# Gated attention with a mixture of experts: three sets of chunks instead of five share their blocks, waits that another wait covers are left out, and VectorE adds four diagonals in every chunk

## The reference

```python
# x, ctx: (128, 64, 128), 8192 tokens of D = 128
def _L0_xattn_ref(q, k, v):      # 16 heads of 8, attention among the 16 heads of one token
    scores = einsum('bsqd,bskd->bsqk', qh, kh) / sqrt(8); scores = where(tril, scores, -1e18)
    return einsum('bsqk,bskd->bsqd', softmax(scores), vh)
def _L0_ffn_ref(x, router_w, experts_bias, w1, w3, w2, sw1, sw3, sw2):   # 8 experts, H = 256
    shared_out = (silu(xf @ sw1) * (xf @ sw3)) @ sw2
    rw, sel = top_k(xf @ router_w.T + experts_bias, 2); rw = softmax(rw)
    moe_out = sum over the two experts: rw * ((silu(xf @ w1[e]) * (xf @ w3[e])) @ w2[e])
    return moe_out + shared_out
x = x + tanh(g_xattn[0]) * _L0_xattn_ref(_layernorm(x), ctx, ctx)
x = x + tanh(g_ffn[0]) * _L0_ffn_ref(_layernorm(x), ...)
```

## Time and profile before

| what | value |
|---|---|
| median of 3 runs | 786.95 us (785.17 to 788.29) |
| profiled execution, its own time | 784.51 us |
| its span in the trace | 782.8 us |
| PE busy | 528.6 us (68%) |
| DVE busy | 523.0 us (67%) |
| POOL busy | 371.2 us (47%) |
| ACT busy | 260.5 us (33%) |
| TensorE clock granted, mean | 0.862 |

### The profile page before, as it was taken

One profiled execution on the slowest core, in us unless ns is written; L12 is line 12 of the kernel. 1 busy time (PEld: TensorE's weight loads), 2 busy tenths in 40 slices (PEclk: granted clock), 3 DMA queues, 4 the chain that ended last, 5 costly groups with the idle time before them and its releaser, 6 DMA issues.

```text
span 782.8 us, 12809 instructions
## 1 busy us (share of the span) xinstructions
PE 528.6 (68%) x3304; PEld 446.3 (57%) x3304; DVE 523.0 (67%) x1290; ACT 260.5 (33%) x618; POOL 371.2 (47%) x377
## 2 busy tenths in 40 slices
PE   0352987889397759875988376817882783785873
PEld 0341576667257646765676346716582773775862
DVE  7889986799798679856997398728982741112121
ACT  1222261516226151614361224404262150331331
POOL 2015047356644746472847476453447064354433
PEclk9976999799799969988999587968997796997996
DMA  7111561054147116524461167721651442679662
GB/s 259 30 54 39 139 197 46 24 162 114 55 121 224 45 47 197 173 86 123 123 208 38 44 183 191 187 79 38 175 145 62 123 132 80 178 202 278 201 187 73
DMA packets 74774, 99.08 MB, mean 127 GB/s; under 512 B 12286, under 2 KB 43922, under 8 KB 74704
## 3 DMA queue, kind: packets, MB, share of 16 engines
q1 hardware_dynamic: 63376, 75.55, 32.5%
q0 software_dynamic: 11040, 22.71, 10.7%
q10 hardware_dynamic: 288, 0.00, 0.0%
HBM read 73.90 MB, written 28.69 MB: 131 GB/s over the span
## 4 chain that ended last, share of the span: by engine, by line
PE 28%; DVE 18%; issue 17%; another core or an unknown queue 13%; SPq 12%; DMA 6%; ACT 4%; POOL 1%; POOLq 0%; ACTq 0%; DVEq 0%
PE ps_g L1024 7%; PE ps_o L967 6%; PE ps_y L1051 5%; DMA xr<-rows_in 4%; SPq L460 4%; SPq L463 3%; SPq L471 3%; DVE prod L666 3%; PE ps_g L1011 3%; PE ps_o L965 3%; DVE pv L698 3%; DVE sc L671 3%; DVE eo L821 2%; ACT xn L877 2%
## 5 line engine op out<-in xcount | busy, mean ns | idle before, releaser
L596 POOL DMA_INDIRECT ybuf<-yr,xr x163 | 182.6, 1120 | 165.2 <-ACT yr L930 118.4
L1051 PE MATMUL ps_y<-w2s,eo 128*128 (+1 forms) x908 | 142.9, 306 | 96.1 <-DVE xo L827 44.9
L1024 PE MATMUL ps_g<-xrT,wq 128*128 128x128 f32 x1304 | 182.0, 297 | 25.2 <-issue 22.5
L1051 PEld LDWEIGHTS ps_y<-w2s,eo 128*128 128x128 f32 x908 | 125.8, 213 | 114.1 <-issue 78.1
L821 DVE TENSOR_TENSOR eo<-sil,ps_g 128x512 f32<-128x512 f32 (+1 forms) x116 | 77.4, 671 | 167.3 <-ACT sil L914 88.6
L1024 PEld LDWEIGHTS ps_g<-xrT,wq 128*128 128x128 f32 x1304 | 173.1, 213 | 26.8 <-issue 23.7
L588 POOL DMA_INDIRECT rows_in<-xn,idx x128 | 131.3, 1026 | 39.3 <-issue 39.0
L914 ACT ACTIVATE sil<-ps_g 128x512 f32<-128x512 f32 (+1 forms) x116 | 67.6, 589 | 174.9 <-remote 62.9
L563 POOL TENSOR_TENSOR rstd<-ve,mhalf 128x8 f32<-128x8 f32 (+1 forms) x18 | 32.6, 1809 | 165.0 <-DVE nmean L646 165.0
L666 DVE TENSOR_TENSOR prod<-xn,ct 128x512 f32<-128x512 f32 (+21 forms) x144 | 93.4, 651 | 2.0 <-issue 2.0
L671 DVE TENSOR_REDUCE sc<-prod 128x64 f32<-128x512 f32 (+21 forms) x144 | 92.8, 648 | 0.0
(11 more groups left out here) (94 smaller groups left out, 403.6 us busy)
## 6 DMA issues: line engine op xcount, KB each, us to landing
wq<-wall SPq DMA_DIRECT2D x163, 256.0 KB
xr<-rows_in SPq DMA_DIRECT2D x163, 65.0 KB
...
ybuf<-yr,xr POOLq DMA_INDIRECT x163
...
```

The source lines that it names most:

```text
L596: pool.indirect_dma_start(ybuf, bass.IndirectOffsetOnAxis(ap=xr_i[:, BLOCK[c, r + a] % XG, D + 1:DW], axis=0), yr[:, i % YR, a], None, bou ...
L1024: last = nc.tensor.matmul(ps_g[n % 2][:, q // HC, q % HC, a * P:(a + 1) * P], wq[:, b % WR, q * P:(q + 1) * P], xrT[:, i % 3, a * P:(a + 1 ...
L1051: last = nc.tensor.matmul(ps_y[:, a * D:(a + 1) * D], eo[:, n % 2, c, a * P:(a + 1) * P], w[:, c * D:(c + 1) * D], start=(c == 0), stop=(c ...
```

## The change

`SETS` becomes three sets instead of five, so `DONE` becomes 1, 16, 16, 30, 9, 16, 16, 30, 15, in all 149 blocks, and SP zeroes three times (after chunks 3, 7 and 8) instead of five (after 0, 3, 6, 7 and 8). VectorE adds diagonals 1, 3, 5 and 7 in all chunks; before it did so in chunks 4 to 8. Waits are left out where an earlier wait of the same engine, or the order on TensorE, already covers them. 19 values of `URG` and `AHEAD` differ, one of them new.

```diff
-    SETS = [[0], [1, 2, 3], [4, 5, 6], [7], [8]]
+    SETS = [[0, 1, 2, 3], [4, 5, 6, 7], [8]]
...
-    ADDED = [[] if c < 4 else [g for g in range(1, 8, 2)] for c in range(CHUNKS)]
+    ADDED = [[g for g in range(1, 8, 2)] for c in range(CHUNKS)]
...
-        URG = {('sp', 'load'): 4.8, ('sp', 'result'): -3.7, ('sp', 'block'): 0.3, ('sp', 'zero'): 3.9,
+        URG = {('sp', 'load'): 1.6, ('sp', 'result'): 3.3, ('sp', 'block'): 0.3, ('sp', 'zero'): 3.9,
...
+    PE_AT = {unit: at for at, unit in enumerate(ORDER["pe"])}
+
+    def on_pe(first, then):
+
+        return PE_AT[first] < PE_AT[then]
+
+    def up_unit(n):
+        return "up" + SEQ[n][0], SEQ[n][1]
...
-                sp.wait_ge(s["tab"], c + 1)
+                if r == 0:
+                    sp.wait_ge(s["tab"], c + 1)
                 at = sp.value_load(table[r:r + 1, c:c + 1], min_val=0, max_val=E * SPAN - 1)
-                if b >= WR:
+                if b >= WR and (b == WR or RPAIR[BLOCKS[b - WR]] > RPAIR[BLOCKS[b - WR - 1]]):
                     sp.wait_ge(s["gu"], PLACE["R", RPAIR[BLOCKS[b - WR]]] + 1)
...
-                sp.wait_ge(s_sc[c % 2], SCATTERED[c])
-                if c in LAST:
-                    sp.wait_ge(s["zeroed"], 16 * (1 + E * (SET[c] + 1)))
-                if b >= XG:
+                if r == 0:
+                    sp.wait_ge(s_sc[c % 2], SCATTERED[c])
+                    if c in LAST:
+                        sp.wait_ge(s["zeroed"], 16 * (1 + E * (SET[c] + 1)))
+                if b >= XG and (b == XG or RPAIR[BLOCKS[b - XG]] > RPAIR[BLOCKS[b - XG - 1]]):
...
                 dve.wait_ge(s["sil"], n + 1)
-                need(dve, s["y"], n - 1)
+                if n >= 2 and not on_pe(("down", n - 2), up_unit(n)):
+                    dve.wait_ge(s["y"], n - 1)
...
                 act.wait_ge(s["gu"], n + 1)
-                need(act, s["eo"], n - 1)
...
-                if i >= 3:
+                if i >= 3 and not on_pe(("upR", i - 3), ("tr", i)):
                     act.wait_ge(s["gu"], PLACE["R", i - 3] + 1)
...
-                need(pe, s["eo"], n - 1)
+                if n >= 2 and not on_pe(("down", n - 2), ("upR", i)):
+                    pe.wait_ge(s["eo"], n - 1)
```

More of the change, by code:

```diff
@@ L95, in planned @@
     def planned():
-        URG = {('sp', 'load'): 4.8, ('sp', 'result'): -3.7, ('sp', 'block'): 0.3, ('sp', 'zero'): 3.9,
+        URG = {('sp', 'load'): 1.6, ('sp', 'result'): 3.3, ('sp', 'block'): 0.3, ('sp', 'zero'): 3.9,
               ('sp', 'back'): 0.5, ('dve', 'ln1a'): 5.8, ('dve', 'scores'): 4.1, ('dve', 'values'): -0.4,
-              ('dve', 'sum'): 2.0, ('dve', 'chain'): -1.4, ('dve', 'eo'): -1.0, ('dve', 'xo'): -0.4,
-              ('dve', 'mix'): 0.5, ('dve', 'tab'): 5.3, ('pool', 'inv1'): 0.6, ('pool', 'inv2'): 2.9,
-              ('pool', 'scatter'): 1.2, ('pool', 'post'): 6.7, ('pool', 'gather'): 3.6, ('act', 'ln1b'): 1.3,
+              ('dve', 'sum'): 2.0, ('dve', 'chain'): 2.3, ('dve', 'eo'): -1.0, ('dve', 'xo'): -0.4,
+              ('dve', 'mix'): -0.6, ('dve', 'tab'): 6.5, ('pool', 'inv1'): 4.9, ('pool', 'inv2'): 2.9,
+              ('pool', 'scatter'): 1.2, ('pool', 'post'): 6.1, ('pool', 'gather'): 3.6, ('act', 'ln1b'): 1.3,
               ('act', 'exp'): 4.9, ('act', 'chain'): 2.9, ('act', 'again'): 5.4, ('act', 'sil'): 4.8,
-              ('act', 'xrT'): 2.6, ('act', 'yr'): 2.6, ('pe', 'sums'): 2.7, ('pe', 'chain'): 0.3,
-              ('pe', 'turn'): 4.0, ('pe', 'upR'): 9.2, ('pe', 'upS'): 6.1, ('pe', 'down'): 5.2}
-        AHEAD = {'tr': 0.8, 'sil': 0.4, 'eo': 0.2, 'upR': 3.0, 'inv2': 1.5, 'scatter': 1.5, 'down': 0, 'upS': 0.2,
-                'scores': 0, 'gather': 0, 'block': 0.4, 'chain': 0.4, 'turn': 0.2, 'post': 0.8, 'back': 0.8,
-                'exp': 0, 'ln1b': 0.4, 'sums': 0, 'inv1': 0.8}
+              ('act', 'xrT'): 2.6, ('act', 'yr'): -0.6, ('pe', 'sums'): 2.6, ('pe', 'chain'): 1.6,
+              ('pe', 'turn'): 3.6, ('pe', 'upR'): 4.5, ('pe', 'upS'): 6.4, ('pe', 'down'): 2.8}
+        AHEAD = {'tr': 0.8, 'sil': 0.4, 'eo': 0, 'upR': 3.0, 'inv2': 0.4, 'scatter': 1.5, 'down': 0, 'upS': 0.2,
+                'scores': 0, 'gather': 0, 'block': 0, 'chain': 0.4, 'turn': 0.2, 'post': 3.0, 'back': 0.8, 'exp': 0,
+                'ln1b': 0.4, 'sums': 0, 'inv1': 0.8, 'sum': 0.4}
         HOP = .15
@@ L1007, in up_shared @@
                     pe.wait_ge(s["w"], 16 * LOADED)
-                pe.wait_ge(s["xntc"], HALVED[c + 1])
-                need(pe, s["eo"], n - 1)
+                if not on_pe(("logit", c), ("upS", j)):
+                    pe.wait_ge(s["xntc"], HALVED[c + 1])
+                if n >= 2 and not on_pe(("down", n - 2), ("upS", j)):
+                    pe.wait_ge(s["eo"], n - 1)
                 for q in range(2 * HC):
@@ L1017, in up_routed @@
                 n = PLACE["R", i]
-                pe.wait_ge(s["turned"], i + 1)
-                need(pe, s["eo"], n - 1)
+                if i + 1 == len(RPAIRS) or not on_pe(("tr", i + 1), ("upR", i)):
+                    pe.wait_ge(s["turned"], i + 1)
+                if n >= 2 and not on_pe(("down", n - 2), ("upR", i)):
+                    pe.wait_ge(s["eo"], n - 1)
                 for a in range(w):
@@ L1032, in look_up @@
                 c, r, w = RPAIRS[i]
-                pe.wait_ge(s["tab"], c + 1)
+                if r == 0:
+                    pe.wait_ge(s["tab"], c + 1)
                 for a in range(w):
```

## The result

The changed kernel takes 762.96 us (median of four runs, 762.09 to 766.18) beside 787.47 us for the kernel before (four runs, 785.17 to 788.29). The ratio is 0.9711, with a 95% interval from 0.967 to 0.9752: faster, by 24.5 us. I had said 772 us, in a range from 752 to 786.

A forecast was written before the change was run, and what follows sets the result against it. VectorE was taken to set attention and SP's issue the tail. Terms: +9.0 - 4 in attention, -5 in the gap, -11.7 - 3 in the tail, +2 at the end, -12.7: 774, lowered by 2 to 772 us; range 752 to 786.

The forecast's parts named there:

- The bound and the tail: Behind the last `zero`, SP's issue sets the pace; 5 blocks fewer at 2.33 us save 11.7 us.
- SP never waits for a buffer there: In the tail of the kernel before, SP's waits on a block's load were read as only 0.6 us.
- The rival in which TensorE sets the tail: Tail: TensorE or transfers set the pace, saving 7.0 us for 11.7 and nothing for waits; 780 us, 13%.
- The waits left out: SP in the tail: 0.1 us a block over 35 blocks, taken as 3 us saved; nothing on other engines.
- The adds: DVE in attention: 13.6 us more for adds in chunks 0 to 3, 4.6 us moved to the tail, net +9.0.
- The rule against the change: Attention: each added DVE add can hold up a POOL issue by its own length; at most 11 us on POOL.
- My own price for POOL's posts beside DVE's adds: Rival: sixteen times 0.7 us of POOL delay reach the path, 11 us more, 783 us; 3%.
- The order: Attention: the new order saves 4 us in sum, -7 + 5.2 + 3 - 5.2, around the scatters.
- The gap: Between attention and the last `zero`'s end: a scatter run of 8 and not 12, 5 us less.
- The end: After the last block: accumulates and results of chunks 4 and 5 now stand there, 2 us more.
- The front frees more: Rival: chunk 2's period falls to 61 us and `zero` time counts, giving 757 us; 25%.
- Longer scatter runs turn the sign: Rival: scatter runs of 16 cost DVE 15 us each in chunks 1 to 3, giving 796 us, slower; 9%.

The follow-up runs named there:

- e3: The changed kernel with one more unused table read on SP in each of the last 35 blocks: 679.74 us, ratio 1.0016.
- e7: The kernel before with the three new sets of chunks alone: 782.8 us, ratio 1.0068.
- e12: The changed kernel with table values on SP and TensorE read without bounds, two steps fewer per read: 749.35 us, ratio 0.9582.
- e1: The changed kernel with SP's waits of a block put back, order the same: 664.5 us, ratio 0.9775.
- e8: The kernel before with the covered waits left out and nothing else: 770.69 us, ratio 0.99.
- e10: The changed kernel with the sixteen adds of chunks 0 to 3 moved from VectorE to TensorE sums, order frozen: 754.5 us, ratio 0.9673.
- e5: The changed kernel again, unaltered, on the chip that has the long waits: 753.24 us, ratio 0.9689.
- e6: The kernel before again, unaltered, on the chip that has the long waits: 781.87 us in one run.
- e11: The changed kernel with four POOL fills amid the scatters of chunks 1 to 7, on the chip with the long waits: 716.87 us, ratio 0.9169.
- e4: The changed kernel with four POOL fills amid the scatters of chunks 1 to 7, on the chip without the long waits: 693.99 us, ratio 1.0223.

## Why the prediction was right, and where a step of it failed

**The bound and the tail: right.** SP's issue sets the tail (e3), fewer blocks behind the last `zero` shorten it (e7: 15.3 us), and SP has no wait there in the kernel after. The size was too small: the pace is 2.00 us a block and not 2.2 to 2.3, so that 19.8 us came where I had 14.7. A reading was wrong here. "SP never waits for a buffer there" came from a table that leaves out a stop of 6.1 us in the kernel before; my 2.33 us a block had it spread over 40 blocks, and that the new sets take it away, by moving the reads and results of chunks behind the last blocks, I had not seen. It is worth about as much as the 5.1 us more that the end then takes. The rival in which TensorE sets the tail is refuted as a price for this change (e3), but it holds for that one stop, and e12 shows it 0.3 us a block further on.

**The waits left out: mis-sized.** On SP 0.07 us a block (e1) against my estimate of 0.1, with no effect on the tail's length that the runs of that chip show. But the step "on the other engines the removed waits were long met: nothing" failed. Alone, the waits are worth 9.6 us by the medians (e8), and 6.9 us of that execution lie in attention. Which engine's waits gave the 6.9 us no run separates, and two profiled executions of one program, the changed kernel, differ by 9.2 us in this stage; so the gain is shown by the medians and its place isn't.

**The adds: overcharged, as far as is known.** I charged all of their 13.6 us because DVE is the busiest engine. Two pairs of runs, in the frozen order, say nearly nothing: 1.6 us of the stage in e10 against e5, with medians 754.5 and 753.24, and on the other chip the run without them was the later one. DVE's busy time did rise by 9.5 us, as worked out (13.6 - 4.6 = 9.0); and its long waits fell by 12.5 us. DVE is busy 78% of the stage, so I could have asked which of its waits the adds would fill. The waits that e10 shows in their place arise in the frozen order and hardly stand in the kernel before (5.5 us), so what the adds cost against that kernel stays open.

**The rule against the change.** My own price for POOL's posts beside DVE's adds was a rival with 3%. Its row was misread: the post of 1.70 us did not run beside an add, but beside two `pv` products:

```profile
547.36 1.89 DVE L698 TENSOR_TENSOR pv<-ex,ct 128x832 f32<-128x832 f32 x2
```

These have two inputs in SBUF as well, so the direction stands. With and without the sixteen adds POOL's posts took 1145 ns each in the mean (e10 and e5), so the delay did not show. The Trainium skill, SBUF — State Buffer, section "SBUF: two separate sides", would have each added add hold up a POOL operation that reads SBUF; in these two runs the sixteen adds left no trace of that.

**The order: a small sum of parts that I did not have.** I had +5 us for attention, from adds and order; it was -0.3 in the result, and -9.3 on the chip of e5 to e12 (e5 beside e6). Alone, on that chip, the sets cost it 17.6 us, the planner's numbers give 12.2 (in an execution 8 us faster than its median) and the waits 6.9: -1.5 together, so some 8 us of the 9.3 belong to no part alone, and none of these is a term of mine. Chunk 1 lost its waits, as I had said; for chunks 2 and 3 I had said 8 to 12 us and they have 2.7 and 9.3 (5.70 + 3.64). What it gained in chunk 6 (12.5 us in two waits for 15.0 and 4.3) I had not seen.

**What the parts are worth together.** By the medians the sets cost 2.5 us, the waits give 9.6, the planner's numbers cost 1.4: 5.7 us of gain in all. By the ratios (1.0068, 0.99, 1.0015) it is 0.17%, some 1.3 us. The three together, without the adds but in an order planned with them, give 25.5 us (e10). So some 20 us of the gain belong to no part alone, within some 6 us to either side by e10's interval. The stages suggest how: the sets pay in the tail only when the order that they bring is not worse ahead of it, and the new numbers are an order for these sets; with the old sets they push work from attention into the gap. My sum treated them as one order, read from the finished program, which was the right unit. That it came out within 10 us of the result is in part luck: attention was 5.3 us off and the tail 5.1, and the parts inside attention (17.6, -12.2 and -6.9 us), which my sum did not have, happened nearly to cancel. Pairs of parts weren't run, so which two carry most of the 20 us stays open.

**The gap and the end.** The gap gave 2.3 us for my 5. The last `zero` met a run of 8 scatters and only two posts, but took 14.1 us and not 11, and DVE's wait behind it was still 10.9 us for 14.4. The end took 5.1 us more than before, and not 2, for the reason that I gave: the results of two chunks stand behind the last block, and SP waits 17.2 us for the accumulates (`xo<-ybuf`) of their rows.

**The other rivals.** "The front frees more" (757 us) is nearer to the measured time than my sum's 772 is, but not for its reason: attention ended within 0.3 us of before, and the tail gave 5.1 us more than I had. "Longer scatter runs turn the sign" decided from 12 us each in chunks 1 to 3, and these had none, 2.7 and 9.3.

**The better version.** e11 beats both kernels on a chip with the waits (716.87 us beside 753.24 and 780.02) and would lose some 4% to the changed kernel on a chip without them (e4's 693.99 beside e1's 664.5). A version with both e11's break and e12's reads was not run.
